# A four-layer graph network on one core: in its last pass, which rows TensorE fetches, and how wide their one-hots are made

## What is computed

```python
f = concat([h[src], h[dst]]);  msg = f @ M_w.T + M_b
ssum = segment_sum(msg, dst);  sq = segment_sum(msg * msg, dst)
mx = segment_max(msg, dst);    mn = segment_min(msg, dst)
# mean, mx, mn, std, each also scaled by log(deg + 1), then @ U_w.T, batch norm
```

## Time and profile before

| | |
|---|---|
| median of three runs | 6750.53 us (6738.99 to 6770.34) |
| profiled execution | 6772.31 us |
| its span | 6770.5 us |
| TensorE clock, mean over the span | 0.772 |
| busy: TensorE, VectorE, ScalarE, GpSimd | 53%, 60%, 38%, 46% |
| DMA, mean over the span | 120 GB/s |

### The profile page before, as it was taken

How to read it: one execution, slowest core, us unless ns; L and a number is a source line. 1 busy time by engine, 2 the same in 40 slices (tenths; PEclk the granted TensorE clock), 3 DMA queues, 4 the chain that set the end, 5 groups by cost and what they waited for, 6 DMA issues and landing times.

```text
span 6770.5 us, 62645 instructions
## 1 busy us (share of the span) xinstructions
PE 3554.9 (53%) x16066; PEld 1798.5 (27%) x16066; DVE 4061.1 (60%) x11179; ACT 2584.5 (38%) x6230; POOL 3089.6 (46%) x3105
## 2 busy tenths in 40 slices
PE   4555765545545366654553654555533333332789
PEld 1111332222222233322222222222221111111444
DVE  8999755555555556655555555555566666667411
ACT  5666033223323233322322332332325666666310
POOL 3444244454444455545445544544526555555100
PEclk9999977777777677877776777777766666666899
DMA  4333612222222233322222322222315555555256
GB/s 137 130 129 130 247 47 85 77 85 86 79 81 87 67 86 92 97 79 83 86 79 63 91 79 81 87 79 80 88 48 183 223 220 216 217 216 221 93 213 242
DMA packets 321453, 814.16 MB, mean 120 GB/s; under 512 B 80530, under 2 KB 237694, under 8 KB 306306
## 3 DMA queue, kind: packets, MB, share of 16 engines
q1 hardware_dynamic: 201234, 594.04, 22.6%
q0 software_dynamic: 92336, 200.10, 12.5%
q10 hardware_dynamic: 27584, 16.53, 1.0%
HBM read 349.01 MB, written 461.41 MB: 120 GB/s over the span
## 4 chain that ended last, share of the span: by engine, by line
DVE 33%; another core or an unknown queue 22%; PE 13%; issue 12%; ACT 9%; DMA 1%; POOL 0%; SPq 0%; DVEq 0%; ACTq 0%; POOLq 0%
DVE big L1682 10%; PE psT L997 5%; DVE big L1598 5%; DVE big L1672 5%; ACT hT L838 3%; DVE big L1622 2%; PE psY L1124 2%; PE psT L1124 1%; DVE big L1695 1%; PE psY L1204 1%; PE psY L1174 1%; DVE big L1678 1%; DVE top_b L1653 1%; DVE m_b L1658 1%
## 5 line engine op out<-in xcount | busy, mean ns | idle before, releaser
L662 POOL DMA_INDIRECT big<-table,src_win x2660 | 2562.1, 963 | 2431.8 <-DVE big L1682 1043.0
L854 ACT ACTIVATE psH<-d_b 128x60 f32<-128x60 f32 x168 | 37.6, 224 | 2318.2 <-DVE d_b L1664 1950.5
L1682 DVE SCALAR_TENSOR_TENSOR big<-big,keep_win 128x132 f32<-128x132 f32 x2184 | 779.0, 357 | 112.6 <-DVE big L1682 26.1
L1146 PE MATMUL psS<-big,hT 128*128 128x384 bf16 x1400 | 354.8, 432 | 803.5 <-DVE hT L1607 803.5
L825 ACT ACTIVATE hT<-src_bc,node_c 128x640 bf16<-128x640 f16 x840 | 621.4, 815 | 284.6 <-remote 150.2
L1124 PE MATMUL psT<-big,hT 128*128 128x408 bf16 x1200 | 388.8, 387 | 466.2 <-DVE big L1622 385.9
L1124 PE MATMUL psY<-big,hT 128*128 128x408 bf16 x1200 | 387.8, 387 | 388.9 <-DVE big L1622 368.3
L1124 PE MATMUL psT<-big 128*128 128x408 bf16 x1800 | 498.4, 341 | 81.9 <-issue 46.8
L1124 PE MATMUL psY<-big 128*128 128x408 bf16 x1800 | 497.8, 340 | 40.0 <-issue 39.6
L830 ACT ACTIVATE hT<-hT 128x3200 bf16<-128x3200 bf16 x168 | 482.2, 2870 | 5.4
L602 POOL TENSOR_SCALAR big<-big 128x400 bf16<-128x400 f16 x198 | 278.0, 1404 | 369.5 <-PE psY L1056 173.1
(11 more groups left out here) (349 smaller groups left out, 7247.5 us busy)
## 6 DMA issues: line engine op xcount, KB each, us to landing
rows<-big SPq DMA_DIRECT2D x112, 1792.0 KB
rows<-big SPq DMA_DIRECT2D x168, 952.0 KB
big<-A_d SPq DMA_DIRECT2D x17, 6400.0 KB, 19.2
A_d<-big SPq DMA_DIRECT2D x396, 200.0 KB, 1.9
big<-table,src_win POOLq DMA_INDIRECT x2660
big<-A_d SPq DMA_DIRECT2D x7, 1600.0 KB, 7.1
src_bc<-pe_src_d ACTq DMA_DIRECT2D x84, 128.0 KB
table<-big SPq DMA_DIRECT2D x15, 350.0 KB
```

The costliest lines, as they stand in the source:

```text
L662: pool.indirect_dma_start(out=rows[:, k, 0:p.table_w], out_offset=None, in_=table, in_offset=bass.IndirectOffsetOnAxis(ap=src_win[:, s, k: ...
L1146: ins = nc.tensor.matmul(psS[:, 0:3 * D].rearrange("p (c w) -> p c w", c=3), is_src[:, t, 0:P], table_s[:, t, :, 0:D], start=(n == 0), sto ...
L1682: v.scalar_tensor_tensor(state[:, k, 0:GATW], prev[k][:, 0:GATW], kw[:, 0, k:k + 1], rows[:, k, 0:GATW], ALU.mult, ALU.add).then_inc(chain ...
```

## The change

It touches only the fourth pass and its preparation.

- dma_steps: GpSimd gathers six rows of every group of the fourth pass; TensorE fetches the seventh of every group, not of the odd ones only.
- The sources of these rows get their own array in DRAM, last_src_d (112 x 128), made by one more cast, transpose, copy and DMA.
- One broadcast brings the sources of all four groups of a round (QH = 512 columns), issued after the store of group 3 for the round after next.
- quad_hots replaces pair_hots. ScalarE makes six tiles (PNA_A), 512 columns wide, in two buffers (quad_a, in hT's memory), after group 1. VectorE makes 19, in one buffer (quad_v, behind the gathered rows), after group 2, and waits there for all four fetches of the round.
- TensorE does 25 matmuls for every group, on 128 of the 512 columns. It waits for the one-hots once a round and for the reduce before every fetch. psS stays the one bank.
- VectorE's reduce and ScalarE's wait for it come in every group.

```diff
-HOT_S = 9
+PNA_A = 6
     def dma_steps(self, s):
-        return self.by_dma - s % 2
+        return self.by_dma - (s % 2 if self.kind == GAT else 1)
...
+        QH = SLOTS * P
+        quad_a = [hT[:].rearrange("f t n -> f (t n)")[:, z * (PNA_A * QH // 2):(z + 1) * (PNA_A * QH // 2)].bitcast(BF16)
+                  .rearrange("p (t e) -> p t e", e=QH) for z in range(2)]
+        AHEAD = SLOTS * passes[3].steps * passes[3].step_w
+        quad_v = words(AHEAD, (NT - PNA_A) * QH // 2).bitcast(BF16).rearrange("p (t e) -> p t e", e=QH)
...
+            sp.dma_start(last_src_d.rearrange("(k p) -> k p", p=P), last_src).then_inc(pe_src_out, 16)
+            sp.wait_ge(pe_src_out, 48)
...
+                def broadcast_last(rnd):
+                    sp.dma_start(src_bc[:, 0, 0:QH], last_src_d[bass.ds(rnd * QH, QH)].partition_broadcast(P)
+                                 ).then_inc(src_bc_in[0], 16)
...
-                        if p.pairs and s % 2 and not final:
-                            broadcast_pair(rnd + 1, s // 2)
+                        if p.pairs and s == SLOTS - 1 and not final:
+                            broadcast_last(rnd + 2)
...
+                def quad_hots(rnd):
+                    act.wait_ge(src_bc_in[0], p.src_bc0 + 16 * (rnd + 1))
+                    if rnd >= 2:
+                        act.wait_ge(fetched, p.halves0 + SLOTS * (rnd - 1))
+                    to = quad_a[rnd % 2]
+                    for t in range(PNA_A):
+                        ins = nc.scalar.activation(to[:, t, :], src_bc[:, 0, 0:QH], ACT.Square,
                                                    bias=node_c[:, t:t + 1], scale=-1.0)
                     ins.then_inc(distant, 1)
+                    act.wait_ge(distant, p.halves0 + rnd + 1)
+                    nc.scalar.activation(to, to, ACT.Relu, bias=1.0, scale=-1.0).then_inc(is_src_rdy, 1)
...
                             if k == p.dma_steps(s):
-                                act.wait_ge(fetched_rdy, p.fetched0 + 2 * rnd + s // 2 + 1)
+                                act.wait_ge(fetched_rdy, p.fetched0 + SLOTS * rnd + s + 1)
...
-                        if s % 2 and not (final and s == SLOTS - 1):
-                            pair_hots(2 * rnd + s // 2 + 1)
+                        if s == 1 and not final:
+                            quad_hots(rnd + 1)
...
-                for q in range(p.groups // 2 if p.pairs else 0):
+                for n in range(p.groups if p.pairs else 0):
+                    rnd, s = n // SLOTS, n % SLOTS
+                    if n == 0:
                         pe.wait_ge(split_rdy, p.splits0 + 5)
                     else:
+                        pe.wait_ge(fetched_rdy, p.fetched0 + n)
+                    if s == 0:
+                        pe.wait_ge(is_src_rdy, p.halves0 + rnd + 1)
+                        pe.wait_ge(is_src_v_rdy, p.halves0 + rnd + 1)
+                    for t in range(NT):
+                        hot = quad_a[rnd % 2][:, t, :] if t < PNA_A else quad_v[:, t - PNA_A, :]
+                        ins = nc.tensor.matmul(psS[:, 0:3 * D].rearrange("p (c w) -> p c w", c=3), hot[:, s * P:(s + 1) * P],
+                                               table_s[:, t, :, 0:D], start=(t == 0), stop=(t == NT - 1))
                     ins.then_inc(fetched, 1)
...
+                def quad_hots(rnd):
+                    dve.wait_ge(src_bc_in[0], p.src_bc0 + 16 * (rnd + 1))
+                    if rnd:
+                        dve.wait_ge(fetched, p.halves0 + SLOTS * rnd)
+                    for t in range(PNA_A, NT):
+                        ins = v.tensor_scalar(quad_v[:, t - PNA_A, :], src_bc[:, 0, 0:QH], node_c[:, t:t + 1], None,
                                               ALU.is_equal)
                     ins.then_inc(is_src_v_rdy, 1)
...
-                    if p.pairs and s % 2:
-                        dve.wait_ge(fetched, p.halves0 + 2 * rnd + s // 2 + 1)
+                    if p.pairs:
+                        dve.wait_ge(fetched, p.halves0 + SLOTS * rnd + s + 1)
                         v.reduce_sum(rows[:, p.steps - 1, :], psS[:, 0:3 * D].rearrange("p (c w) -> p w c", c=3),
                                      mybir.AxisListType.X).then_inc(fetched_rdy, 1)
...
-                        if s % 2 and not (final and s == SLOTS - 1):
-                            pair_hots(2 * rnd + s // 2 + 1)
+                        if s == SLOTS - 2 and not final:
+                            quad_hots(rnd + 1)
```

More of the change, by code:

```diff
@@ L533, in store @@
                                      state_rows(p, s % ROWS_SLOTS)).then_inc(rows_out[s % ROWS_SLOTS], 16)
-                        if p.pairs and s % 2 and not final:
-                            broadcast_pair(rnd + 1, s // 2)
-                with sp.Fori(0, p.rounds - 1, 1) as rnd:
-                    store(rnd)
+                        if p.pairs and s == SLOTS - 1 and not final:
+                            broadcast_last(rnd + 2)
+                if p.pairs:
+                    with sp.Fori(0, p.rounds - 2, 1) as rnd:
+                        store(rnd)
+                    store(p.rounds - 2, final=True)
+                else:
+                    with sp.Fori(0, p.rounds - 1, 1) as rnd:
+                        store(rnd)
                 store(p.rounds - 1, final=True)
@@ L1396, in lanes @@
                                 src_i[:].rearrange("p (g n) -> p g n", n=14)[:, :, 12:14], -float(MID), None, ALU.add)
+                v.tensor_scalar(lane_x[:, 2, 0:PS], src_i[:].rearrange("p (g n) -> p g n", n=7)[:, :, 6], -float(MID),
+                                None, ALU.add)
                 v.tensor_scalar(lane_x[:, 1, 0:PO], src_i[:].rearrange("p (g n) -> p g n", n=28)[:, :, 25], -float(MID),
@@ L1708, in _ @@
                 if p.pairs:
-                    pair_hots(0)
+                    quad_hots(0)
                 for s in range(SLOTS):
```

47 lines of the change are left out of this document (13 added, 34 removed).

## The result

The forecast was 6665 us; the kernel after takes **6863.1 us** (median of four runs, 6821.6 to 6873.9), against 6744.8 for four runs of the kernel before taken with it (6728.6 to 6770.3). The ratio is 1.0155, with a 95% interval of 1.0119 to 1.019: slower, outside the range. The profiled execution after took 6863.2 us, its span 6861.3; the one before 6772.3.

What follows compares the result with a forecast made beforehand. A chain of waits, no full engine, was taken to bound the fourth pass. Rounds of 38.3 us made it 1079 against 1164.6 us, 86 less; with 1 us of preparation, 6665 us against the median, range 6540 to 6810.

Steps and rivals of the forecast that it cites:

- The sum by VectorE and ScalarE: Fourth-pass round added up along these two engines: 38.05 us; the path by TensorE came out equally long.
- reduce 0 to reduce 1: Fourth-pass round, from the first group's reduce to the second's: 8.0 us, as in the kernel before.
- reduce 1 to the one-hots: Round, second reduce to the end of group 2's updates, ScalarE's one-hots (6.5 us) included: 14.2 us.
- F1: First fetch of a fourth-pass round, after 8 to 9 us of idle: 9.6 us to its reduce, as before.
- One-hots: Wide one-hots, once a round: VectorE's 19 take 5.5 us with gaps, ScalarE's six and the Relu 6.5 us.
- Gathers: Fourth pass: 56 of 728 gathers go, 70 us of GpSimd, costed at nothing because its wait already covers it.
- The second to fourth fetch: Later fetches of a round: 4.2 us by the records plus 2.6 us late arrival, 6.8 us each.
- Clock: TensorE's granted clock in the fourth pass rises from 0.65 to above 0.8; later fetches run at 1.00.
- no change: Rival: the clock stays low, or ScalarE's rows come late in two groups; 6760 to 6780 us or near; chance 0.19.
- The slower one: Rival: with the single PSUM bank each fetch takes 9.6 us, round 46.45 us, time 6893 us; chance 0.20.
- Faster by more: Rival: fetch lateness goes where GpSimd is silent, round 33.2 us, time 6523 us; chance 0.16.
- the signs: Profile after: 112 reduces, 38.3 us period, clock above 0.8, one-hots 5 to 5.5 and 6.5 us, GpSimd idle share holding or growing.

Runs made afterwards that it cites:

- the pieces: Kernel after with VectorE's 19 wide one-hots cut into four pieces among the third group's updates and the fourth's start: ratio 1.0013, on the faster occasion 1.0095.
- one gather of six: Kernel after with only the first of each fourth-pass group's six gathers issued, the other rows stale: 6501.2 us.
- fetch of odd groups: Kernel after with its wide one-hots, but TensorE fetching only for odd groups and GpSimd gathering 7 and 6 rows by turns: ratio 1.0232; in another set 6946.5 us.
- moved call: Kernel after with VectorE's wide one-hots made behind the fourth group's reduce instead of the third group's updates: ratio 0.9996, when run again 1.0119.
- ScalarE's narrow rows: Kernel after with ScalarE's three row instructions 8 columns wide in place of 128, the rest stale: 6835.0 us.

## Why the prediction was wrong

The sum by VectorE and ScalarE can be laid beside the trace term by term. A round is counted here from its first fetch to that of the next; "behind a held one" are the 13 rounds whose one-hots were made in a block that held a gather, "others" 13 more, with the first left out:

| Term | forecast | measured, mean | behind a held one | others |
|---|---|---|---|---|
| first fetch to its reduce | 9.6 | 10.8 | 8.7 | 13.2 |
| reduce 0 to reduce 1 | 8.0 | 12.8 | 18.1 | 7.6 |
| reduce 1 to the one-hots | 14.2 | 14.5 | 14.8 | 14.3 |
| one-hots to reduce 3 | 5.5 | 5.4 | 5.8 | 5.0 |
| reduce 3 to the next fetch | 0.75 | 0.6 | 0.6 | 0.6 |
| round | 38.05 | 44.1 | 48.0 | 40.7 |

So the miss of 6 us lies in two terms, "reduce 0 to reduce 1, as now" (4.8 us) and F1 (1.2 us), and the first of them is off only where a held gather came before; F1 is off in the other rounds.

- **One-hots: right.** 19 on VectorE were to take 5.1 to 5.5 us and took 5.07 beside a held gather and about 5.8 beside free ones, 5.45 in the mean; ScalarE's six and Relu were to take 6.5 and took 3.77 + 2.76. VectorE waits in group 2 for its rows, 0.4 and 2.3 us by turns where I said 3. The third and fourth terms together are right to 0.2 us.
- **Gathers: the step that failed first.** I cost the 56 gathers at nothing, since GpSimd's waits covered them, and wrote that no sum came near GpSimd's 30 us a round. It looked only at how many gathers there are, not at what stops one. The wide one-hots held gathers for 14 x 4.7 = 66 of the 70 us that GpSimd was spared, and at the worst place. The cut of those instructions to 128 columns removed that altogether, the pieces all but 0.85 us a time, and the pieces took the loss down to 1.0013 with it.
- **The second to fourth fetch, 6.8 each: wrong in kind.** I read the lateness as an amount, 2.6 us. It goes with the gathers that GpSimd issues beside the fetch, as the table below shows. Two of the three came out better than forecast, and the trace of before held the hint: the fetches at its start and end, with few gathers, were late by 1.5 us or less, which I took for a reason to keep an amount.
- **Clock: half right.** The loop's clock rose to 0.75, not above 0.8. Slot 3, and slot 2 in every other round, follow idle stretches of 0.7 to 1.8 us and run at full speed (25 matmuls in 4.2 us). Slot 0 always starts low, after 8 to 9 us of idle; slot 1 mostly does, and slot 2 in the rounds behind a held gather, after 10 to 17 us. (In the kernel before it is not 8 to 9 us, as I wrote: the earlier trace rows have 13.4 and 14.7.) The Trainium skill's rule on short idles ("TensorE: Matmul & The Clock Gate", A second HAM failure mode), which speaks of a clock that goes to and fro and which I priced as no change, decided nothing: the fetches with 0.7 to 1.8 us of idle before them ran at 1.00.
- **The rivals.** The slower one (a single bank with F = 9.6) named the right end by a wrong mechanism: fetch 1 alone is far over 8 us, the mean of the three is 8.0, and a second bank did not help. "Faster by more" described the free rounds' slots 2 and 3 well (5.3 us where GpSimd is silent), and missed that the gathers it clears there pile up beside slots 0 and 1.
- **Of the signs** I named, 112 reduces, the 6.5 us and, in half of the rounds, one-hots of 5 to 5.5 us came; GpSimd's idle share grew as I said (busy 55% in place of 58), and that hid the held time within the busy one; the clock over 0.8 and the 38.3 us did not; "wrong if the second to fourth fetch take over 8 us" was met by the second.

How late a fetch is, by slot: from its first matmul to its reduce in us, and in brackets how long GpSimd was inside gathers meanwhile (means of the rounds in the traces, counted as in the table above):

| Kernel | slot 0 | slot 1 | slot 2 |
|---|---|---|---|
| after, the other rounds | 13.2 (7.4) | 7.0 (4.1) | 5.3 (1.0) |
| after, rounds behind a held gather | 8.7 (6.7) | 17.5 (10.7) | 7.2 (0) |
| one gather of six | 6.6 (0.9) | 5.3 (0.9) | 5.4 (0) |
| pieces, where before takes 5153 us | 7.0 (5.2) | 5.3 (3.9) | 5.3 (4.0) |

The first two rows give the 44.1 us their shape (the 7.2 us of slot 2 are no lateness: its 25 matmuls take 7.1 us there, at the low clock). A gather held for 4.7 us in group 2 pushes the rest of its row into slot 1 of the next round, 10.7 us of gathers beside one fetch. That fetch takes 17.5 us and VectorE stands still for 10 of them. By this account 4.7 us of GpSimd's time cost 5.7 us of the round, and the next round, its gathers early again, is free. That the pile-up makes this difference is read from these means; it was not tested by itself. The last row shows that gathers alone don't make a fetch late; the occasion is needed too.

Net, the change brought nothing on either occasion even without the held gathers. Where fetches are late, four fetches and 24 gathers take 41.3 us (the pieces), two and 26 take 41.2 to 41.8, and none and 28 take 41.1 (each from a set of its own). What holds all three at 41 us there stays open; that fetches and gathers hinder each other can't be the whole of it, since the last has no fetch. Where they aren't late, the 2.5 us a round that GpSimd gained meet VectorE's chain of some 34 us, of which 29 are work.

## What to carry to other kernels

Before widening a VectorE instruction or making a longer block of them, look at what GpSimd issues at that moment, and ask for the longest of its gathers in the trace, not only the mean: here 14 of 660 carried the whole loss and the mean rose by 0.1 us. Keep such blocks short (five instructions held a gather for under 1 us more, nineteen for 4.7), and count the held gathers in more than one execution before trusting a placement, since the phase decides: the same moved call had 4 and 18. And when an engine is late for a reason that no record shows, split its lateness by what else runs, slot by slot, before carrying it over as a constant.

## What was not expected of the hardware

- *Which gathers are held.* In the kernel after, the 14 that started 0.43 or 0.44 us ahead of the block were held, 5.63 us each; five that started 0.20 to 0.24 us ahead were not, nor any further ahead or inside it. With the fetch of odd groups all 25 between 0.14 and 0.46 us ahead were held. With the moved call some at 0.16 to 0.36 us behind the block's start were held as well, 4.8 to 5.0 us, and some were not. The block is 19 instructions, and the gather waits for all of them. With ScalarE's narrow rows, 15 gathers that started 0.13 to 0.30 us ahead were held and some at 0.22 to 0.40 us were not. In the earlier passes, blocks of 7 to 15 instructions of 640 columns stood beside 380 gathers and held none of them; the long gathers there, six of 3.0 to 3.5 us, stood beside float32 instructions on two operands of 3136 and 3200 columns:

```profile
3711.74 3.49 DVE L1598 TENSOR_TENSOR xt<-xt,rowb 128x3200 f32<-128x3200 f32 x1
3712.63 3.42 POOL L679 DMA_INDIRECT big<-table,src_win  x1 [0.30 <-issue]
```

  So it takes neither two-byte operands nor a block of many instructions to hold a gather. Why most gathers inside a block get through is open.
- *Two occasions.* Instruction durations are the same, 5150 and 6760 us are not. Clearest is a strict exchange between ScalarE and TensorE at the end of the third pass: 25 copies, one for each matmul. First the kernel before, then the one that fetches odd groups in its 5265 us set:

```profile
L918 ACT COPY big<-psY x25: 272/273/278, 3591.1 to 3624.8; 128x136 f32<-128x136 f32 x25
```

```profile
L935 ACT COPY big<-psY x25: 272/273/273, 3622.0 to 3633.4; 128x136 f32<-128x136 f32 x25
```

  A copy takes 0.27 us in both; 24 exchanges take 33.7 us in one and 11.4 in the other, both with gathers beside them. The slow one doesn't start slow. Its first ten copies follow each other by 0.45 and 0.73 us in turn, as they do at the start of the other trace; then the distances grow to 1.4, 2.1, 2.8 and 4.2 us, and they are 1.0 us or less again from 3623.2 on, 4 us after the last gather has ended:

```profile
3596.26 0.27 ACT L918 COPY big<-psY 128x136 f32<-128x136 f32 x1 [0.18 <-issue]
3602.04 0.27 ACT L918 COPY big<-psY 128x136 f32<-128x136 f32 x1 [1.85 <-PE psY L1174]
3617.56 0.27 ACT L918 COPY big<-psY 128x136 f32<-128x136 f32 x1 [3.96 <-remote]
3624.84 0.27 ACT L918 COPY big<-psY 128x136 f32<-128x136 f32 x1 [0.18 <-PE psY L1174]
...
3617.89 0.95 POOL L676 DMA_INDIRECT big<-rows,end_i  x1 [0.30 <-issue]
```

  So TensorE and ScalarE lose time between instructions, not in them, on one occasion and not on the other, with the same chip showing both; the loss grows while GpSimd gathers without a break, and ends after it. The Trainium skill ("SBUF — State Buffer", Who interferes with whom) has it that "PE and ACT never wait on anyone". That is said of the ports of SBUF, and the equal 0.27 us agree with it; what the engines wait for between instructions (their next instructions, a semaphore's event, or something else) no view shows and no run separates. What makes the occasion stays open, and so does why descriptors are enough for it.
